# A graph network in one kernel: the mean's division moved into the subtraction, the variance's and epsilon into ScalarE's root

## The reference

```python
def _layernorm(x, axis=-1, eps=1e-05):
    m = jnp.mean(x, axis=axis, keepdims=True)
    v = jnp.var(x, axis=axis, keepdims=True)
    return (x - m) / jnp.sqrt(v + eps)

h = jnp.maximum(_layernorm(x), 0.0); x = x + L0(h, src, dst)             # degree-normed sum over edges
h = jnp.maximum(_layernorm(x), 0.0); x = x + L1(h, edge_index, theta)    # sum of theta[k] * (Laplacian)^k h
h = jnp.maximum(_layernorm(x), 0.0); x = x + L2(h, weights, etype)       # relational attention, relu
h = jnp.maximum(_layernorm(x), 0.0); x = x + L3(h, src, dst)             # 10 steps: h = 0.9 * A h + 0.1 * h0
```

## Time and profile before

| | |
|---|---|
| median of 3 runs | 2788.61 us |
| the profiled execution | 2789.32 us, of which the span is 2779.9 us |
| DVE busy | 1768.5 us (64%), 3130 instructions |
| POOL busy | 1800.6 us (65%), 1786 |
| PE busy | 430.6 us (15%), 2105 |
| ACT busy | 335.7 us (12%), 1043 |
| DMA | 77.00 MB, 28 GB/s over the span |

### The profile page before, as it was taken

One profiled execution on the slowest core, in us unless ns is written; L12 is line 12 of the kernel. 1 busy time (PEld: TensorE's weight loads), 2 busy tenths in 40 slices (PEclk: granted clock), 3 DMA queues, 4 the chain that ended last, 5 costly groups with the idle time before them and its releaser, 6 DMA issues.

```text
span 2779.9 us, 14498 instructions
## 1 busy us (share of the span) xinstructions
PE 430.6 (15%) x2105; PEld 214.1 (8%) x2105; DVE 1768.5 (64%) x3130; ACT 335.7 (12%) x1043; POOL 1800.6 (65%) x1786
## 2 busy tenths in 40 slices
PE   0000000000010000000000098294195000006000
PEld 0000000000010000000000033031131000006000
DVE  8998896666679967177766678587878921420000
ACT  0000021111100110011111144141042200000000
POOL 6666677777554471575777456766456777466776
DMA  1001022221100130110301100100000120000000
GB/s 20 15 11 26 15 61 50 50 50 31 28 9 6 62 127 22 33 57 20 101 25 18 18 3 4 11 2 6 5 7 8 62 63 10 29 11 7 11 8 8
DMA packets 68026, 77.00 MB, mean 28 GB/s; under 512 B 34799, under 2 KB 60872, under 8 KB 67192
## 3 DMA queue, kind: packets, MB, share of 16 engines
q0 software_dynamic: 56384, 23.45, 6.4%
q1 hardware_dynamic: 5720, 27.38, 2.5%
q10 hardware_dynamic: 5856, 25.60, 2.4%
HBM read 35.67 MB, written 46.87 MB: 30 GB/s over the span
## 4 chain that ended last, share of the span: by engine, by line
DVE 49%; issue 25%; POOL 9%; PE 7%; another core or an unknown queue 6%; DMA 2%; ACT 2%; DVEq 1%; POOLq 0%; ACTq 0%; SPq 0%
POOL out L1568 8%; DVE mf L520 7%; DVE pay L520 4%; DVE z L520 3%; DVE psum L915 3%; DVE outs L520 2%; DVE psum L523 2%; PE psum L2009 2%; DVE mf L902 2%; DVE xs L902 2%; DVE xs L897 2%; PE psum L2010 2%; DVE st L544 1%; DVE mf L897 1%
## 5 line engine op out<-in xcount | busy, mean ns | idle before, releaser
L1562 POOL DMA_INDIRECT xs<-in_x,i_src x196 | 200.0, 1020 | 131.2 <-issue 53.9
L1568 POOL DMA_INDIRECT out<-outs,i_outS x196 | 205.2, 1047 | 117.3 <-issue 60.8
L1562 POOL DMA_INDIRECT xd<-x_rows,i_dstX x196 | 204.6, 1044 | 112.5 <-DVE z L1374 66.7
L1562 POOL DMA_INDIRECT xd<-in_x,i_dst x196 | 205.2, 1047 | 111.2 <-DVE mf L520 42.6
L1562 POOL DMA_INDIRECT mf<-x_rows,i_srcX x196 | 200.5, 1023 | 94.5 <-issue 64.3
L1568 POOL DMA_INDIRECT out<-outs,i_srcX x196 | 196.3, 1001 | 71.5 <-issue 58.9
L1562 POOL DMA_INDIRECT pay<-payload_by_dst,i_rank x196 | 195.1, 996 | 62.6 <-issue 62.6
L520 DVE TENSOR_TENSOR mf<-mf 128x128 f32<-128x128 f32 (+5 forms) x578 | 175.1, 341 | 12.2 <-DVE mf L520 1.9
L520 DVE TENSOR_TENSOR pay<-psum,pay 128x512 f32<-128x512 f32 x196 | 132.5, 688 | 66.5 <-ACT pay L1887 56.2
L2009 PE MATMUL psum<-pay 64*128 64x512 f16 x196 | 117.4, 599 | 117.2 <-ACT pay L1872 77.3
L1932 PE MATMUL psum<-ident,small 128*128 128x128 f32 x4 | 1.6, 501 | 851.2 <-DVE small L960 851.2
(11 more groups left out here) (458 smaller groups left out, 2479.9 us busy)
## 6 DMA issues: line engine op xcount, KB each, us to landing
z<-in_x ACTq DMA_DIRECT2D x14, 624.0 KB
out<-z ACTq DMA_DIRECT2D x14, 624.0 KB
l_first_rows<-mf SPq DMA_DIRECT2D x2, 3234.0 KB, 9.7
outs<-in_x ACTq DMA_DIRECT2D x6, 624.0 KB
out<-outs ACTq DMA_DIRECT2D x6, 624.0 KB
l_own_rows<-pay SPq DMA_DIRECT2D x1, 3626.0 KB, 11.0
payload_by_dst<-z SPq DMA_DIRECT2D x1, 3234.0 KB
x_rows<-z SPq DMA_DIRECT2D x1, 3234.0 KB
```

Source lines behind the costliest of these rows:

```text
L1562: G.indirect_dma_start(out=dest(k), out_offset=None, in_=table, in_offset=bass.IndirectOffsetOnAxis(ap=idx[:, k:k + 1], axis=0), bounds_ch ...
L1568: G.indirect_dma_start(out=table, out_offset=bass.IndirectOffsetOnAxis(ap=idx[:, k:k + 1], axis=0), in_=source(k), in_offset=None, bounds_ ...
```

## The change

The norm's first sum stays undivided; the subtraction becomes one scalar_tensor_tensor, (sum x -1/D) + x. The two sums of squares go straight into `sq_in`; the second one signals ScalarE, and ScalarE's activation computes the root of (sum x 1/D + EPS), with epsilon as bias from a new tile `eps`. In the dense part the same is done, and in its third layer ALPHA goes into the root as well: the root of (sum / (D x ALPHA^2) + EPS / ALPHA^2), whose reciprocal is ALPHA times the old one. The root of degrees (`root`) keeps its copy.

```diff
+        eps = sb("eps", 2)
...
             def layernorm(xin, hout, tmp, w=EC):
 
-                m, v = c["st1"][:, 0:w], c["st2"][:, 0:w]
-                mean, scale = MEAN[:, 0:w], SCALE[:, 0:w]
+                squares = c["sq_in"]
+                total, scale = MEAN[:, 0:w], SCALE[:, 0:w]
                 sides = (slice(0, w // 2), slice(w // 2, w))
-                link(V.tensor_reduce(m, xin, AX.X, ALU.add))
-                link(ts(mean, m, 1.0 / D, None, ALU.mult))
+                link(V.tensor_reduce(total, xin, AX.X, ALU.add))
                 for side in sides:
-                    tt(tmp[:, side, :], xin[:, side, :], bc(mean[:, side]), ALU.subtract).then_inc(s["norm_centred"], 1)
-                for k, side in enumerate(sides):
-                    dve.wait_ge(s["norm_squared"], 2 * norms[0] + k + 1)
-                    link(V.tensor_reduce(v[:, side], hout[:, side, :], AX.X, ALU.add))
-                link(ts(v, v, 1.0 / D, EPS, ALU.mult, ALU.add))
-                root_main(link, scale, v, w)
+                    V.scalar_tensor_tensor(out=tmp[:, side, :], in0=bc(total[:, side]), scalar=-1.0 / D, in1=xin[:, side, :],
+                                           op0=ALU.mult, op1=ALU.add).then_inc(s["norm_centred"], 1)
+                root_count[0] += 1
+                dve.wait_ge(s["norm_squared"], 2 * norms[0] + 1)
+                link(V.tensor_reduce(squares[:, sides[0]], hout[:, sides[0], :], AX.X, ALU.add))
+                dve.wait_ge(s["norm_squared"], 2 * norms[0] + 2)
+                V.tensor_reduce(squares[:, sides[1]], hout[:, sides[1], :], AX.X, ALU.add).then_inc(s["root_in"], 1)
+                dve.wait_ge(s["root_out"], root_count[0])
+                link(V.reciprocal(scale, c["sq_out"][:, 0:w]))
...
+            link(V.memset(eps[:, 0:1], EPS))
+            link(V.memset(eps[:, 1:2], EPS / ALPHA ** 2))
...
@@ dense_pair
-                        chain(V.tensor_reduce(dst1[b][0:pn, 0:cn], X3, AX.X, ALU.add))
-                        chain(ts(dense_m[b][0:pn, 0:cn], dst1[b][0:pn, 0:cn], 1.0 / D, None, ALU.mult))
-                        tt(rows(dxc[b][0:pn, 0:w]), X3, bc(dense_m[b][0:pn, 0:cn]), ALU.subtract).then_inc(s["dense_xc"], 1)
+                        chain(V.tensor_reduce(dense_m[b][0:pn, 0:cn], X3, AX.X, ALU.add))
+                        V.scalar_tensor_tensor(out=rows(dxc[b][0:pn, 0:w]), in0=bc(dense_m[b][0:pn, 0:cn]), scalar=-1.0 / D, in1=X3,
+                                               op0=ALU.mult, op1=ALU.add).then_inc(s["dense_xc"], 1)
                     for b in range(nb):
                         dve.wait_ge(s["dense_sq"], number(l, b))
-                        chain(V.tensor_reduce(dst2[b][0:pn, 0:cn], rows(dsq[b][0:pn, 0:w]), AX.X, ALU.add))
-                        ts(dst2[b][0:pn, 0:cn], dst2[b][0:pn, 0:cn], 1.0 / D, EPS, ALU.mult, ALU.add).then_inc(s["dense_var"], 1)
+                        V.tensor_reduce(dst2[b][0:pn, 0:cn], rows(dsq[b][0:pn, 0:w]), AX.X, ALU.add).then_inc(s["dense_var"], 1)
...
-                        if l == 2:
-                            chain(ts(scale, scale, ALPHA, None, ALU.mult))
...
-            PER = 2 * 2 * (3 * 5 + 2 + 2)
+            PER = 2 * 2 * (3 * 3 + 2 + 1)
...
@@ ScalarE, norm
-                root(1)
+                roots[0] += 1
+                act.wait_ge(s["root_in"], roots[0])
+                S.activation(c["sq_out"][:, 0:w], c["sq_in"][:, 0:w], ACT.Sqrt, bias=eps[:, 0:1], scale=1.0 / D).then_inc(s["root_out"], 1)
...
@@ ScalarE, dense_act
-                        S.activation(dst3[b][0:pn, 0:cn], dst2[b][0:pn, 0:cn], ACT.Sqrt).then_inc(s["dense_root"], 1)
+                        S.activation(dst3[b][0:pn, 0:cn], dst2[b][0:pn, 0:cn], ACT.Sqrt, bias=eps[0:pn, l // 2:l // 2 + 1],
+                                     scale=1.0 / (D * (ALPHA ** 2 if l == 2 else 1.0))).then_inc(s["dense_root"], 1)
```

More of the change, by code:

```diff
@@ L534, in roots, with root @@
                 return root
-            root_main = roots("root_in", "root_out")
-            norms, feeds = [0], [0]
+            root_count, norms, feeds = [0], [0], [0]
+            def root(o, a):
+                root_count[0] += 1
+                V.tensor_copy(c["sq_in"][:, 0:EC], a).then_inc(s["root_in"], 1)
+                dve.wait_ge(s["root_out"], root_count[0])
+                link(V.reciprocal(o, c["sq_out"][:, 0:EC]))
             def layernorm(xin, hout, tmp, w=EC):
-                m, v = c["st1"][:, 0:w], c["st2"][:, 0:w]
-                mean, scale = MEAN[:, 0:w], SCALE[:, 0:w]
+                squares = c["sq_in"]
+                total, scale = MEAN[:, 0:w], SCALE[:, 0:w]
                 sides = (slice(0, w // 2), slice(w // 2, w))
-                link(V.tensor_reduce(m, xin, AX.X, ALU.add))
-                link(ts(mean, m, 1.0 / D, None, ALU.mult))
+                link(V.tensor_reduce(total, xin, AX.X, ALU.add))
                 for side in sides:
-                    tt(tmp[:, side, :], xin[:, side, :], bc(mean[:, side]), ALU.subtract).then_inc(s["norm_centred"], 1)
-                for k, side in enumerate(sides):
-                    dve.wait_ge(s["norm_squared"], 2 * norms[0] + k + 1)
-                    link(V.tensor_reduce(v[:, side], hout[:, side, :], AX.X, ALU.add))
-                link(ts(v, v, 1.0 / D, EPS, ALU.mult, ALU.add))
-                root_main(link, scale, v, w)
+                    V.scalar_tensor_tensor(out=tmp[:, side, :], in0=bc(total[:, side]), scalar=-1.0 / D, in1=xin[:, side, :],
+                                           op0=ALU.mult, op1=ALU.add).then_inc(s["norm_centred"], 1)
+                root_count[0] += 1
+                dve.wait_ge(s["norm_squared"], 2 * norms[0] + 1)
+                link(V.tensor_reduce(squares[:, sides[0]], hout[:, sides[0], :], AX.X, ALU.add))
+                dve.wait_ge(s["norm_squared"], 2 * norms[0] + 2)
+                V.tensor_reduce(squares[:, sides[1]], hout[:, sides[1], :], AX.X, ALU.add).then_inc(s["root_in"], 1)
+                dve.wait_ge(s["root_out"], root_count[0])
+                link(V.reciprocal(scale, c["sq_out"][:, 0:w]))
                 norms[0] += 1
@@ L580, in layernorm_of @@
                 chain(V.scalar_tensor_tensor(out=hout, in0=tmp, scalar=0.0, in1=bc(m), op0=ALU.max, op1=ALU.mult))
-            def root(o, a):
-                root_main(link, o, a)
             link(V.memset(xd_t[:], 0.0))
             link(V.memset(xs_t[:], 0.0))
+            link(V.memset(eps[:, 0:1], EPS))
+            link(V.memset(eps[:, 1:2], EPS / ALPHA ** 2))
             for n in ("kp0", "kc0", "kn", "et"):
```

## The result

The kernel after took 2764.31 us in the median of 5 runs (2761.4 to 2772.83), the kernel before 2788.61 beside it (5 runs, 2783.84 to 2793.77): a ratio of 0.9917, interval 0.9894 to 0.9941. The sign and the range of the forecast held; of the 69 us forecast, 24 came. The profiled execution took 2764.31 us, 9.3 of them outside the span.

What follows compares the result with a forecast made beforehand. Neither DVE nor POOL fills the span; a quarter of the chain is "issue", with paced stretches of one DVE instruction per 1.4 us. -25 - 3 - 11 - 1.5 - 26 - 2.7 = -69; 2789.3 - 69 = 2720, range 2640 to 2768.

Steps and rivals of the forecast that it cites:

- Paced and free layers: Dense part: paced layers take one DVE instruction per 1.4 us, 16.8, 19.6 and 16.8 us; halves 0 to 3 gain 72.
- the idle moves on: Rival for paced stretches: long instructions meet the delay once small ones go; only durations gained, 38 us, 2751; chance 0.18.
- the port mechanism: Small DVE operations wait for POOL's running instruction; about 99 us gained, nothing paid in the listing, 2690; chance 0.05.
- The listing: Behind halves 0 to 3: DVE comes at 694, is paced until near 768; of 79 us ahead, 25 are left.
- The lower bound: Low end for the listing: paced until 800, 4 us left of the 79.
- From the listing to layer 2: Half 4 with the norm behind it gains 11 us, half 5 with its paced scans 1.5.
- Halves 6 to 9 and the turns: Turns of layer 2 could begin 46 us earlier, but begin in earnest near 1569 as POOL stops; 26 kept.
- up to the norm of 196 columns: First stages through the listing and the norms behind it: 25 us left at the listing, 3 from norms.
- from tile 71 to the end: Four norms before the later turns gain 2.7 us; the last two norms nothing.
- Rival 3: Listing and sums paced to their end, +38 us; turns held past 1570; whole kernel 44 us slower, 2833; chance 0.07.

Runs made afterwards that it cites:

- b_rows130: The kernel before with ROWS_AT_ONCE 130 instead of 60, so POOL's gathers of xs are not held back; 2863.36 us, 1.0233 to the kernel before.
- again_rows20: The kernel after with ROWS_AT_ONCE 20 instead of 60 (free rows of xs); 2754.76 us, 0.9849 to the kernel before.
- rows0: The kernel after with ROWS_AT_ONCE 0 instead of 60, so no free row of xs; 2759.51 us, 0.9852 to the kernel before.
- again_after: The kernel after, unchanged, run once more in a later group; 2778.99 us, 0.9939 to the kernel before.

## Why the forecast was wrong, step by step

- **Paced and free layers**: right. 16.3, 19.6 and 17.3 us against 16.8, 19.6 and 16.8; halves 0 to 3 won 81 us where 72 stood; POOL's payload (666.89) was just hidden. The rivals "the idle moves on" and the port mechanism are out: paced layers are counted in slots of 1.4 us, memsets that nobody waits for included. By the Trainium skill's rule (SBUF — State Buffer, "Who interferes with whom") a DVE form that takes the ports shared with POOL waits for a POOL instruction that holds them; that doesn't explain these traces, for in `b_rows130` DVE is paced for 24 us with a single POOL instruction among them.
- **The listing**: the step that failed. I let the pace end about 765 because a paced DVE starves POOL, so that 25 of 79 us stayed; POOL was starved (11 issues from 780 to 820), and the pace stayed until 815. I had read its end from the earlier trace rows, 4 us behind POOL; elsewhere it is 17 us (`again_rows20`, behind the issue at 716), 24 (`rows0`) and 28 (`b_rows130`), and here POOL's last issue of the dense run is at 777.51, some 37 us ahead of the end. The lower bound, 4 us left of 79 if paced until 800, was the case that came: of 92 us at the listing's start none was left at the norm of 196 columns (937.45, where it was 936.13).
- **From the listing to layer 2**: half 4 was right (-14.7 us at the copy behind it, against -11). Half 5 and its scans were put at -1.5; they and half 6 brought POOL's part 0 forward by 21 us in all (1275.25 instead of 1296.08), and less in `again_after`, whose scans are paced.
- **Halves 6 to 9 and the turns**: on POOL's clock DVE came 74 us earlier where 46 stood, for halves 8 and 9 stayed free, which no term of mine had; 7 were kept where 26 stood. Mechanism right, size wrong by the same step: I let the turns begin in earnest as POOL stops, and they are held some 15 to 20 us more behind 1561.22.
- **The sum**, by stages, in us:

| | forecast | measured |
|---|---|---|
| up to the norm of 196 columns | -28 | +1.3 |
| from there to part 0 of layer 2 | -12.5 | -22 |
| halves 6 to 9 and the turns, up to tile 71 | -26 | -7 |
| from tile 71 to the end | -2.7 | +2.7 |
| sum | -69 | -25 |

The first and the third row are the tail of the pace, 48 us; the others go the other way or are small. Rival 3 had the right mechanism for the listing (paced past 800), but paced to its end, for +38.

Open: what the pace is, what sets its beginning and its end. That it depends on the chip, and comes with 9.3 us outside the span instead of 1.7, says that it is not the kernel's instructions alone; whether the recording of the trace has a part in it no run tells.

## What to carry to other kernels

Where starts of small instructions stand on a fixed grid beside long runs of indirect DMAs, each instruction costs a slot there whatever its length, so count instructions, and look at what is ready when the stretch ends: an engine that comes early into such a stretch arrives with it, not ahead of it. A gain in front of a stage whose end is set by another engine or by a clock is given back whole; measure halves of a change, not only the whole. And run before and after on more than one chip before 1% decides: the change was worth 0.8 and 0.6% in two groups of runs with the pace, and its halves 0.2% each on the one without.

## What the runs showed of the hardware

- One kernel, two chips, 2790 and 2507 us; the slots of 1.4 us are on the one and not on the other, at the same granted clock of 1.0 and a POOL period of 1.32 to 1.33 us in the payload on either.
- Beside POOL's run from 1277 or 1282 the pace started once DVE had used up some 20 to 25 instructions beyond one per 1.4 us; in the sort of keys 67 beyond it brought none. It outlasted POOL's issues by 4 us, 17, 24 and 28 us.
- A memset of one column behind each indirect DMA on POOL left 164 of 195 periods at 1.30 us and raised the mean from 1.33 to 1.41, since POOL itself was held in ten short stretches; the dense stretch beside it was free.
